# A graph network on one core: what GpSimd waits for before it reuses a gather buffer

## The reference

```
e = edge_attr @ enc_edge_w + enc_edge_b
msg = relu(h[src] + e) + 1e-7
m = msg * t
ex = exp(m - segment_max(m, dst)[dst])
alpha = ex / (segment_sum(ex, dst)[dst] + 1e-16)
agg = segment_sum(msg * alpha, dst)
z = relu(layernorm((h + agg) @ w1 + b1))
out = z @ w2 + b2
```

## Time and profile before

| | us |
|---|---|
| median of 3 runs | 5297.16 |
| the three runs | 5278.94 to 5298.56 |
| the profiled execution | 5282.58 |
| its span, first to last instruction | 5280.6 |
| PE busy | 2419.4 |
| DVE busy | 2887.4 |
| ACT busy | 1842.4 |
| POOL busy | 3084.4 |

### The profile page before, as it was taken

How to read it: one execution, slowest core, us unless ns; L and a number is a source line. 1 busy time by engine, 2 the same in 40 slices (tenths; PEclk the granted TensorE clock), 3 DMA queues, 4 the chain that set the end, 5 groups by cost and what they waited for, 6 DMA issues and landing times.

```text
span 5280.6 us, 39054 instructions
## 1 busy us (share of the span) xinstructions
PE 2419.4 (46%) x9927; PEld 1638.7 (31%) x9927; DVE 2887.4 (55%) x3862; ACT 1842.4 (35%) x3505; POOL 3084.4 (58%) x3248
## 2 busy tenths in 40 slices
PE   2566666765334444434433444344442443444444
PEld 1344444443322222223222222232232232222223
DVE  3566666666335555555634555555552555555555
ACT  1344443444223333333322333333332333333334
POOL 4666666653466666666355666666625666666661
PEclk8677676777566766666656667666665666666675
DMA  2344443434123333333313333333321333333332
GB/s 56 106 115 118 116 124 112 121 112 130 41 75 102 97 106 96 102 101 98 96 41 83 105 98 100 101 97 104 96 80 46 100 98 102 96 106 99 96 103 67
DMA packets 419248, 506.78 MB, mean 96 GB/s; under 512 B 184319, under 2 KB 190201, under 8 KB 419004
## 3 DMA queue, kind: packets, MB, share of 16 engines
q1 hardware_dynamic: 312398, 393.85, 23.2%
q0 software_dynamic: 103552, 109.52, 10.8%
q10 hardware_dynamic: 3054, 0.71, 0.1%
HBM read 216.36 MB, written 287.39 MB: 95 GB/s over the span
## 4 chain that ended last, share of the span: by engine, by line
another core or an unknown queue 43%; issue 18%; ACT 17%; DVE 11%; PE 10%; DVEq 1%; POOL 1%; ACTq 0%; DMA 0%; SPq 0%; POOLq 0%
PE pT L774 3%; ACT r L576 3%; ACT decay L583 3%; ACT sw_out L591 3%; DVE M L1057 2%; ACT pX L579 2%; PE pA L744 2%; DVE S L1071 2%; ACT u L578 2%; DVE W L1075 1%; DVE pR L1059 1%; DVE pR L1061 1%; PE pX L763 1%; PE pX L758 1%
## 5 line engine op out<-in xcount | busy, mean ns | idle before, releaser
L495 POOL DMA_INDIRECT zsrc<-z_rows,idx_all x3136 | 2986.9, 952 | 1864.3 <-issue 960.3
L774 PE MATMUL pT<-ident,S 128*128 128x128 f32 x1568 | 568.5, 377 | 2156.8 <-issue 1085.7
L1057 DVE TENSOR_TENSOR_SCAN M<-pR,M,u 128x512 f32<-128x512 f32 x392 | 502.3, 1281 | 1624.2 <-ACT u L578 1522.6
L774 PEld LDWEIGHTS pT<-ident,S 128*128 128x128 f32 x1568 | 337.0, 215 | 2229.9 <-issue 2198.4
L576 ACT ACTIVATE r<-pX 128x512 f32<-128x512 f32 x392 | 233.4, 595 | 2176.8 <-remote 1923.2
L1071 DVE TENSOR_TENSOR_SCAN S<-decay,S,pX 128x512 f32<-128x512 f32 x392 | 501.5, 1279 | 491.6 <-issue 369.8
L758 PE MATMUL pX<-e_in,ident 128*128 128x512 f32 x784 | 697.6, 987 | 118.1 <-ACT e_in L570 91.2
L763 PEld LDWEIGHTS pX<-ident,zsrc 128*128 128x128 f32 x3136 | 566.5, 253 | 405.8 <-issue 325.2
L591 ACT ACTIVATE sw_out<-pT 128x512 f32<-128x512 f32 x784 | 439.5, 589 | 713.4 <-issue 381.0
L763 PE MATMUL pX<-ident,zsrc 128*128 128x128 f32 x3136 | 540.5, 330 | 67.2 <-DMA zsrc<-z_rows,idx_all 67.2
L774 PE MATMUL pT<-ident,W 128*128 128x128 f32 x1568 | 541.4, 359 | 0.0
(11 more groups left out here) (175 smaller groups left out, 1968.7 us busy)
## 6 DMA issues: line engine op xcount, KB each, us to landing
sw_rows<-sw_out SPq DMA_DIRECT2D x784, 256.0 KB
e_in<-e_cols SPq DMA_DIRECT2D x300, 256.0 KB
zsrc<-z_rows,idx_all POOLq DMA_INDIRECT x3136
max_cols<-M SPq DMA_DIRECT2D x392, 128.0 KB
attr_in<-in_edge_attr_dram SPq DMA_DIRECT2D x196, 128.0 KB
e_cols<-e_in SPq DMA_DIRECT2D x98, 256.0 KB
z_rows<-z SPq DMA_DIRECT2D x25, 125.0 KB
node_sw<-sw_rows,row_idx POOLq DMA_INDIRECT x100
```

Source lines behind the costliest of these rows:

```text
L495: pool.indirect_dma_start(zsrc[c % RING][:, t4, h, :], None, z_rows, bass.IndirectOffsetOnAxis(idx_all[:, h, t4, c:c + 1].bitcast(U32), 0) ...
L774: last = pe.transpose(pT[b][:, at:at + P], scanned[c % 2][:, t4:CH:SUB], ident[:, :])
L1057: v.tensor_tensor_scan(M[s][:, 1:CH + 1], pR[s][:, :], u[s][:, :], M[s1][:, CH:CH + 1], ALU.add, ALU.max).then_inc(m_done, 1)
```

## The change

POOL no longer waits for `x_mm` before it reuses a gather buffer. In layers 1 to 3 it waits until the load of the same chunk's edge embedding has landed (`e_loaded`, 16 per load); this implies that `x_mm` has counted chunk c - 7, since SP issues the load only then. In layer 0, which has no such load, it waits for `r_done` of chunk c - 7, ACT's relu of that chunk. Nothing is changed on the other engines.

```diff
@@ -487,9 +487,12 @@
                 pool.sem_inc(pool_passed, 1)
                 g0 = value(pool, l * NCH)
                 for c in range(NCH):
-                    if c >= RING or not first_layer:
-                        pool.wait_ge(x_mm, done(g0 + (c - RING)))
+                    if not first_layer:
+
+                        pool.wait_ge(e_loaded[c % RING], (l - 1) * (16 * USES) + 16 * (c // RING + 1))
                         pool.sem_inc(pool_passed, 1)
+                    elif c >= RING:
+                        pool.wait_ge(r_done, done(g0 + (c - RING)))
                     for h in range(2):
                         for t4 in range(SUB):
                             pool.indirect_dma_start(
```

## The result

The changed kernel takes 5494.35 us (median of 4 runs, 5482.47 to 5506.21); the kernel before took 5290.49 us in the same comparison (4 runs, 5278.94 to 5298.56). The ratio is 1.0387, 95% interval 1.0351 to 1.0423: 3.9% slower. The sign is the forecast one. The size is not: the forecast was 369 us more, the runs show 204 us more and the two profiled executions 199.9 us (5482.47 less 5282.58). That is outside the likeliest case's own range (5580 to 5740 us) and in the rival "partly carried" (5340 to 5570 us).

The account below looks back on a forecast made before the run. TensorE's signals, held while POOL gathers without pause, were taken to bound the kernel. Layers 1 to 3 (324 us) plus layer 0 (45 us) gave 369 us more, forecast 5658 us, own range 5580 to 5740 us; 5220 to 5750 us about 8 in 10.

Parts of the forecast that it names:

- likeliest case: Whole kernel: the added waits are carried in full, 369 us more, 5658 us, 7% slower; chance 0.56.
- partly carried: Rival: only part of the added wait lengthens the cycle, 77% or lower, 5340 to 5570 us; chance 0.15.
- What bounds the kernel now: Cycle of two chunks, 23.64 us: PE's signals are held while POOL gathers without pause, let through some 3 us after 16.
- The landing, 2.4 us: Layers 1 to 3: POOL's start moves later by one 256 KB load's landing, 2.4 us, between 2.24 and 2.64.
- Once per pause, 135 pauses: Layers 1 to 3: only the first of a cycle's two loads delays POOL; 135 x 2.4 = 324 us.
- 100% carried: Every cycle: a delay ahead of the row of gathers moves everything behind it, so all 369 us count.
- The test from the earlier trace (77%): Second gather 0.99 us late lengthened relu to relu by 0.76 us; as lower case 284 us, 5574 us.
- Layer 0, 0.6 us x 75 = 45 us: Layer 0: POOL waits for the relu's end in place of `x_mm`, starting 0.6 us later in 75 pauses, 45 us.
- Signals on time: Rival: POOL's pending wait on PE's semaphore holds the signals; without it they come promptly, 4600 to 4850 us; chance 0.07.
- More chunks per pause: Rival: a signal slips through early in the row, a cycle holds three chunks, faster, 5240 us; chance 0.09.
- Not carried: Rival: the let-through is paced by something other than POOL's start, 5283 to 5297 us; chance 0.07.
- a pause at each chunk: Rival: the second load comes late too, 2.7 us more on 264 chunks, some 6000 us; chance 0.06.

Follow-up runs that it names:

- last experiment: Kernel before, but POOL waits one chunk ahead: `x_mm` of chunk c - 1 in layers 1 to 3, `r_done` of it in layer 0: 6012.48 us, ratio 1.1406.
- built alone: Kernel before, but in layers 1 to 3 POOL waits for the load SP issues behind `x_mm` of chunk c - 1: 6358.31 us, ratio 1.4639.
- experiments with pauses by construction: Kernel before, but layers 1 to 3 wait on chunk c - 1's `x_mm`, its `m_done`, or the load behind its `x_mm`: 5578.96, 6373.93, 6358.31 us.
- first set of experiments: Against the kernel before (4343.72 us): layer 0's new wait alone, layers 1 to 3's alone, `m_done` or `r_done` for the load: ratios 0.9998, 0.9998, 0.9997, 0.9998.

## Why the prediction was right in sign and wrong in size

**What bounds the kernel now: right for the late condition, which was not known to be one of two.** In the compared executions the cycle is pause, signals, gathers, pause, as the earlier trace rows had it. The last experiment supports the reading that pauses keep the signals from being late. It also narrows it: in the first 1.7 us of a row they aren't late either. Nothing in one profile showed that the same kernel can also run with its signals on time, at 4344 us and bound by POOL's issue. The rule that the prediction weighed (the Trainium skill, TensorE: Matmul & The Clock Gate, "The cost: per-tile semaphore tail") models the tail at under 0.1 us; the 0.04 us from add_nodes to the relu agrees with it in the prompt condition, and the 9.3 us of the late one don't.

**The landing, 2.4 us: too small by 0.22 us.** Gather behind relu went from 0.76 to 3.38 us in the mean, 2.62 us; built alone it measured 2.68 us. The upper end of the prediction's reading of the earlier trace rows, 2.64 us, would have been the right choice. The prediction also gave an estimate of 2.6 us by the Trainium skill (DMA: Bandwidth & Descriptors, the fit of fixed and variable cost), and both measurements agree with it, though the page fitted transfers that GpSimd issues and this load is SP's.

**Once per pause, 135 pauses: right.** There are 132, and in the 103 rows of 16 gathers the second load of a pair caused no pause. At 2.62 us the term would be 346 us.

**100% carried: this is the step that failed.** The prediction saw "nothing that could" catch up on a delay ahead of the row. The experiments with pauses by construction confirm this half: where each start follows a signal that PE gives in the pause, 100% is carried. But in the late condition the signal on which a pause ends was mostly given during the row, and how late it is isn't fixed to POOL's start. In the changed kernel it came in the mean 1.03 us earlier against the row's end, in 18 cases before that end. So 346 us became 211 us, 61%. The caveat stood in the rival: "lower where a part of the added pause lets a held signal through". The test from the earlier trace rows (77%) was the better guide than the argument against it.

**Layer 0, 0.6 us x 75 = 45 us: wrong, it is 5 us.** The 0.6 us of the relu are real, but the 0.75 us from signal to gather were not kept. Before, the wait is followed by an operation of its own (`pool_passed`); now it is a constant wait on the gather itself, which starts 0.27 us behind the relu's end (0.87 - 0.60). The prediction named this ("the 0.75 us between signal and gather could shrink a little") and priced it at nothing; it is worth 0.48 us a pause. The last experiment bears this out with 0.12 us a pause (0.87 - 0.75), and the semaphore operation is the likely price: behind signals of PE and of DVE alike (the kernels with `x_mm` and `m_done` of chunk c - 1) the gather starts 0.77 us after the update, behind this constant wait 0.26 us. 75 x 0.12 = 9 us is what that leaves. That the layer grew by 4.7 us is in part chance: its pauses of at least 1.4 us went from 70 to 79 and from 209 to 238 us in all, while the gathers themselves took 14 us less (765 to 751 us busy) and shorter gaps 10 us less. No run shows why.

**The sum.** 346 - 136 + 5 - 16 (mostly between the layers) = 199 us, against 199.9 us between the profiled executions. All four terms are read from the same two traces, so this shows that nothing is missing, and tests no cause.

**The rivals.** *Signals on time* fell: in the changed kernel POOL waits on no PE semaphore, and the relu still waits 1788.9 us for a signal without a named sender (1923.2 us before), so POOL's pending wait isn't what holds them. *More chunks per pause*: 14 rows of 23 or 24 do occur, but with 3.8 us and more from row's end to relu, and 11 rows of 8 stand against them. *Not carried* and *a pause at each chunk* didn't occur. *Partly carried* is what happened; at 0.15 its chance was too low.

**What stays open.** What makes PE's signals late during gathers on some occasions and not on others: a chip of the same number stood beside 4343.72 us in the first set of experiments and beside 5266.89 us in the last. What sets the moment at which a late signal arrives: from POOL's start to the relu it took 22.9 us in the median before (5% to 95%: 22.8 to 23.7), and 22.3 us after, spread from 12.3 to 34.9. And how the two halves of the change, or `m_done` in place of the load, do in the late condition: their kernels ran in the prompt one only, so the 61% rests on one changed kernel.

## What to carry to other kernels

To replace a wait on an early signal by one on a later event costs the whole lateness if the waiting engine pauses for it and the signal itself is prompt, and nothing if the event is long past when the engine asks for it: the same edit cost 3.9% where POOL paused 132 times, and nothing where it never did. So count the pauses in the profile first, and multiply them by what one start comes later, signal to instruction; where the signals themselves arrive late, expect only part of it (here 61%). And ask for a second profile from another occasion before a kernel is tuned around late signals, since a profile shows one condition only.

## What the runs showed of the hardware that was not expected

- The same program took 5254 to 5299 us on some occasions and 4338 to 4358 us on others, with one core in use. On the first, TensorE's signals reach ACT, SP and POOL late (9.3 us behind add_nodes in the earlier trace rows) when POOL has issued indirect gathers back to back for long: in the cycle looked at in layer 2 one given 10.2 us into a row passed at once, those given from 13.6 us on arrived together, 3.2 us behind the row's end. On the other occasions they come 0.04 us behind add_nodes, with the same gathers at 1.25 us each.
- With POOL kept one chunk ahead (8 gathers, then a pause in which add_nodes ends, 3.6 us behind them) the late condition costs a layer nothing: it takes 1388.5 us in the late and 1387.4 us in the prompt condition. Signals given in the first 1.7 us of a row pass at once there.
- A constant wait that stands on the gather itself lets it start 0.27 us behind the end of the relu that it waits for; with a semaphore operation between the wait and the gather it starts 0.75 us behind the start of the relu that the same signal releases, or 0.77 us behind the update.
- A load of 256 KB put between a signal and POOL's gather delays it by 2.68 us, from the issue on.
